# Two FFN blocks around a linear attention: part of five attentions done five phases later, Gelu factors and the residual sum on GpSimd, places for each engine

## What is computed

```python
x = x + 0.5 * ffn(layernorm(x))
x = x + linear_attention(layernorm(x))
x = x + 0.5 * ffn(layernorm(x))

def ffn(x):                       # the same weights both times
    q, k, v = heads(x @ Wq), heads(x @ Wk), heads(x @ Wv)      # 16 heads of 16
    attn = softmax(einsum('bqd,bkd->bkq', q, k) / sqrt(256))   # 1024 x 1024, over q
    z = unheads(einsum('bkq,bkv->bqv', attn, v)) @ Wo
    z = l2_normalize(l2_normalize(z) @ Wff)
    return gelu(z)

def linear_attention(x):          # 8 heads, no softmax
    q, k, v = (x @ w_qkv.T + b_qkv) split in three and by heads
    return ((q @ k.T) @ v) @ w_o.T + b_o
```

## Time and profile before

| | |
|---|---|
| median of three runs | 2874.6 us (2874.1 to 2875.76) |
| span of the profiled execution, first to last instruction | 2872.9 us |
| busy PE / DVE / ACT / POOL | 93% / 93% / 94% / 30% of the span |
| mean granted TensorE clock | 0.984 |
| phases 1 to 8 (with a linear attention) | 182.3 to 184.2 us each |
| phases 9 to 14 | 167.8 to 167.9 us each |
| phase 0, phase 15 | 165.0 and 162.8 us |
| ahead of the first tile, behind the last | 40.6 and 27.2 us |

### The profile page before, as it was taken

How to read it: one execution, slowest core, us unless ns; L and a number is a source line. 1 busy time by engine, 2 the same in 40 slices (tenths; PEclk the granted TensorE clock), 3 DMA queues, 4 the chain that set the end, 5 groups by cost and what they waited for, 6 DMA issues and landing times.

```text
span 2872.9 us, 87477 instructions
## 1 busy us (share of the span) xinstructions
PE 2670.2 (93%) x35680; PEld 1071.4 (37%) x35680; DVE 2667.4 (93%) x5390; ACT 2713.4 (94%) x5031; POOL 862.2 (30%) x1383
## 2 busy tenths in 40 slices
PE   6899999999999999999999999999989899899987
PEld 2233443434434344343443443333333333233432
DVE  5999998998989989999898999999999999999997
ACT  4999999999999999999999999999999999999998
POOL 2324204343143331432324313132331313233121
PEclk9999999999999999999999999999999999999999
DMA  5331242313422334123341243432324343232440
GB/s 125 55 80 30 50 102 53 81 33 60 105 40 53 74 60 104 32 54 81 60 98 30 51 92 60 92 61 57 79 45 103 60 90 61 51 87 43 89 89 16
DMA packets 151587, 192.90 MB, mean 67 GB/s; under 512 B 34129, under 2 KB 85841, under 8 KB 151186
## 3 DMA queue, kind: packets, MB, share of 16 engines
q1 hardware_dynamic: 150802, 186.52, 31.6%
q0 software_dynamic: 384, 0.79, 0.2%
HBM read 36.18 MB, written 16.78 MB: 18 GB/s over the span
## 4 chain that ended last, share of the span: by engine, by line
PE 35%; ACT 30%; DVE 27%; issue 6%; SPq 1%; DMA 0%; POOL 0%; DVEq 0%; ACTq 0%; POOLq 0%
ACT exp_ring L627 24%; DVE exp_ring L712 23%; PE ring L818 12%; PE ring L872 10%; PE o_acc L883 10%; ACT w_xn L638 2%; PE ring L928 2%; ACT xn_T L646 1%; ACT kq_stage L661 1%; DVE bn_stats L752 1%; ACT ring L633 1%; DVE w_xn L729 1%; ACT L638 1%; ACT L627 1%; DVE v_now L785 1%
## 5 line engine op out<-in xcount | busy, mean ns | idle before, releaser
L712 DVE TENSOR_SCALAR_CACHE_REDUCE exp_ring<-ring 128x1024 f32<-128x1024 f32 x2048 | 2409.7, 1214 | 114.4 <-PE ring L872 105.9
L627 ACT ACTIVATE exp_ring<-exp_ring,neg_max 128x1024 f32<-128x1024 f32 x2048 | 2333.0, 1143 | 84.6 <-DVE exp_ring L712 82.0
L872 PE MATMUL ring<-kq_stack 128*32 128x512 bf16 x16384 | 1176.0, 384 | 120.6 <-DVE exp_ring L712 82.1
L883 PE MATMUL o_acc<-exp_ring,v_scaled 128*32 128x512 f32 x8192 | 1080.1, 600 | 32.3 <-POOL v_scaled L580 22.7
L872 PEld LDWEIGHTS ring<-kq_stack 128*32 128x32 bf16 x16384 | 405.6, 96 | 1035.5 <-DVE exp_ring L712 415.7
L580 POOL TENSOR_TENSOR v_scaled<-v_now,exp_rsums 128x64 f32<-128x64 f32 x512 | 149.9, 293 | 1762.5 <-DVE exp_rsums L722 1745.2
L627 ACT ACTIVATION_READ_ACCUMULATOR exp_ring<-exp_ring,neg_max 128x1 f32 x2048 | 387.8, 189 | 0.0
L883 PEld LDWEIGHTS o_acc<-exp_ring,v_scaled 128*32 128x32 f32 x8192 | 252.5, 111 | 251.3 <-POOL v_scaled L580 40.1
L818 PE MATMUL ring<-ffn_wo_wowff,o_T 128*32 128x256 f32 x4096 | 244.2, 380 | 15.2 <-DVE o_T L719 13.9
L818 PE MATMUL ring<-xn_T,ffn_wqkv 128*32 128x512 f32 x2048 | 249.6, 608 | 8.1 <-DVE exp_ring L712 6.7
L818 PEld LDWEIGHTS ring<-ffn_wo_wowff,o_T 128*32 128x32 f32 x4096 | 132.3, 110 | 126.1 <-DVE exp_ring L712 26.1
(11 more groups left out here) (99 smaller groups left out, 1244.1 us busy)
## 6 DMA issues: line engine op xcount, KB each, us to landing
kq_stack<-kq_parts SPq DMA_DIRECT2D x2028, 64.0 KB, 2.4
x_post<-in_L_attn_x SPq DMA_DIRECT2D x8, 1024.0 KB, 8.8
x_slots<-x_post SPq DMA_DIRECT2D x8, 1024.0 KB, 5.5
x_prep<-x_slots SPq DMA_DIRECT2D x8, 1024.0 KB, 9.2
x_post<-x_slots SPq DMA_DIRECT2D x8, 1024.0 KB, 5.8
x_prep<-in_L_attn_x SPq DMA_DIRECT2D x7, 1024.0 KB, 9.1
out<-x_post SPq DMA_DIRECT2D x7, 1024.0 KB, 5.7
x_prep<-in_L_attn_x SPq DMA_DIRECT2D x2, 512.0 KB, 4.6
```

The lines of the kernel that those rows point to most:

```text
L627: nc.scalar.activation(e, e, ACT.Exp, bias=negmax[:, i % NM:i % NM + 1], scale=-1.0, accum_out=sums[:, g % EG, c:c + 1]).then_inc(exp_done, 1)
L712: nc.vector.tensor_scalar(E[:, (g % EG) * HQ + c, :].rearrange("p (b n) -> p b n", b=NB), ps, -1.0, None, ALU.mult, ALU.min, accum_out=neg ...
L872: last = mm(ps[k:k + COLS, n, :], kq[:, 0, c, j * P + k:j * P + k + COLS], kq[:, 1, c, n * BANK:(n + 1) * BANK], start=True, stop=True)
L883: last = mm(O[32 * c:32 * c + 32, n, :], vsc[a][:, g % EG, c, :], E[:, (g % EG) * HQ + c, n * BANK:(n + 1) * BANK], start=(a == 0 and j == ...
```

## The change

1. **Second parts later.** Batches 0 to 2 keep their linear attention in one phase (LINEAR, phases 1 to 3). For batches 3 to 7 phases 4 to 8 (FIRST) do it up to H; x_post (x1), H and the bias row are stored in DRAM, and the mean and factor of the second normalization stay in SBUF in one of six places. In phases 9 to 13 (SECOND), when x1 of the phase's own FFN is stored, SP loads x1, H and the bias of batch p-6; POOL normalizes again (`xn3`, the instruction of `xn2`), and `xt2`, `xbias`, `y` and the store follow (`save_y`). PLAIN is left for phases 0, 14 and 15.
2. **Gelu.** The factors are no longer ACT's scale: behind w_norm POOL multiplies w_xn by both factors, one instruction for each of 8 token tiles, and one Gelu instruction does 128 x 2048 (128 x 1024, twice, in the tail).
3. **Residual sum on POOL.** For each of four chunks it halves w_xn in place and adds it to x_post.
4. **Places.** Each engine has its own table of places, also for every single recip and av step; LEAD and GAP are gone. xt is copied by the engine in whose table it stands: DVE in FIRST, SECOND and PLAIN, ACT in START and LINEAR. z and v: ACT in LINEAR and FIRST, DVE in the others.
5. Small ones: the nbk row is gone, its product is done in T.

```diff
+    NOW = 3
+    LATER = B - 2
...
+LATE = ("load_x1", "load_h", "xn3", "xt2", "xbias", "y", "save_y")
...
+        if 1 <= p <= B:
+            return "LINEAR" if p <= NOW else "FIRST"
+        return "SECOND" if B < p <= PHASES - NOW else "PLAIN"
...
+        if kind in LATE and p > B:
+            return p - LATER
+        return p - 1 if p >= 1 else None
...
+            for kind, places in table(p).get(engine, {}).items():
+                parts = PARTS.get(kind, 1) if engine == "pe" else 1
+                for n, place in enumerate(places):
+                    q = work_of(kind, p, n // parts)
+                    if q is not None:
+                        placed.append((p * TILES + place, len(placed), (kind, q, n // parts), n % parts))
...
-    ON_ACT = {step for place, step in steps if step[0] in ("z", "v") and 1 <= place // TILES <= B}
+    ON_ACT = {step for step, _ in ORDER["act"] if step[0] in ("z", "v", "xt")}
...
+                elif kind == "save_x1":
+                    sp.wait_ge(x1_done, chunk(p, CHUNKS - 1))
+                    sp.dma_start(tokens(x1s[p]), xr[:]).then_inc(stored, 16)
+                elif kind == "load_x1":
+                    sp.wait_ge(stored, stored_before((kind, p, i)))
+                    sp.dma_start(xr[:], tokens(x1s[p])).then_inc(xr_loaded, 16)
+                elif kind == "save_h":
...
+                    sp.dma_start(hs[p], H[:].rearrange("p c d -> p (c d)")).then_inc(h_saved, 16)
+                    sp.dma_start(bs[p], biasw[:]).then_inc(h_saved, 16)
+                elif kind == "load_h":
...
+                    sp.dma_start(H[:].rearrange("p c d -> p (c d)"), hs[p]).then_inc(h_loaded, 16)
+                    sp.dma_start(biasw[:], bs[p]).then_inc(h_loaded, 16)
+                elif kind == "save_y" or kind == "store" and is_linear(p):
...
+                elif kind in ("xn2", "xn3"):
+                    if kind == "xn2":
+                        pool.wait_ge(rstd2_ready, (p + 1) * 2)
+                    else:
+                        pool.wait_ge(xr_loaded, xr_count("load_x1", p))
+                        pool.wait_ge(x1_done, chunk(p + LATER - 1, CHUNKS - 1))
+                    k = kept(p)
+                    nc.gpsimd.tensor_scalar(wb[:, i, 0:D], xr[:, i, :], negm2[:, k, i:i + 1], rstd2[:, k, i:i + 1],
                                             ALU.add, ALU.mult).then_inc(xn2_ready, 1)
...
-                    nc.gpsimd.tensor_tensor(gsc[:, c], ssw[:, c], unorm[:, c], ALU.mult).then_inc(norm_step, 1)
+                    for t in range(NT)[c]:
+                        nc.gpsimd.tensor_scalar(wb[:, t, 0:D], wb[:, t, 0:D], ssw[:, t:t + 1], unorm[:, t:t + 1],
+                                                ALU.mult, ALU.mult).then_inc(w_scaled, 1)
+                elif kind == "x1":
+                    rows = slice(i * CT, (i + 1) * CT)
+                    pool.wait_ge(gelu_done, chunk(p, i))
+                    nc.gpsimd.tensor_scalar(wb[:, rows, 0:D], wb[:, rows, 0:D], 0.5, 0.0, ALU.mult, ALU.add
+                                            ).then_inc(x1_half, 1)
+                    pool.wait_ge(xr_loaded, xr_count("load_xr", p))
+                    pool.wait_ge(x1_half, chunk(p, i))
+                    nc.gpsimd.tensor_tensor(xr[:, rows, :], xr[:, rows, :], wb[:, rows, 0:D], ALU.add
+                                            ).then_inc(x1_done, 1)
...
-                    act.wait_ge(norm_step, (p + i + 1) * 5)
-                    for c in range(NT)[norm_cols(p, i)]:
-                        last = nc.scalar.activation(wb[:, c, 0:D], wb[:, c, 0:D], ACT.Gelu,
-                                                    scale=gsc[:, c:c + 1])
...
+                    c = norm_cols(p, i)
+                    act.wait_ge(w_scaled, p * NT + c.stop)
+                    nc.scalar.activation(wb[:, c, 0:D], wb[:, c, 0:D], ACT.Gelu
+                                         ).then_inc(gelu_done, (c.stop - c.start) // CT)
...
-                elif kind == "x1":
-                    dve.wait_ge(xr_loaded, (p + 1) * 16)
-                    dve.wait_ge(gelu_done, chunk(p, i))
-                    rows = slice(i * CT, (i + 1) * CT)
-                    nc.vector.scalar_tensor_tensor(out=xr[:, rows, :], in0=wb[:, rows, 0:D], scalar=0.5,
-                                                   in1=xr[:, rows, :], op0=ALU.mult, op1=ALU.add
-                                                   ).then_inc(x1_done, 1)
...
+                elif kind == "xt" and (kind, p, i) not in ON_ACT:
+                    if p >= 1:
+                        dve.wait_ge(filled["qk"], nth("pe", "qk", p - 1, 7))
+                        dve.wait_ge(filled["v"], nth("pe", "v", p - 1, 3))
+                    nc.vector.tensor_copy(XT[:, i, :].rearrange("p (b n) -> p b n", b=NB), ps).then_inc(xt_out["dve"], 1)
```

581 lines of the change are left out of this document (393 added, 188 removed), and 50 rows, old and new, of the table TABLES.

## The result

The changed kernel takes **2801.53 us** (2799.59 to 2802.07, four runs) where the kernel before took 2874.35 us on the same chip: a ratio of 0.9747, 95% interval 0.9735 to 0.9758, or 72.8 us less. The forecast was 2834.6 us, with a range from 2805 to 2861. The time lies 3.5 us under the range, and the gain is nearly twice the 40.0 forecast.

A forecast was written before the change was run, and what follows sets the result against it. PE was taken to bound phases 1 to 8, ACT and DVE nearly equally 9 to 14. Terms -52.3 + 11.8 - 2.4 - 2 + 1 - 3 + 6.9 = -40.0 us from 2874.6 gave 2834.6, range 2805 to 2861.

The forecast's parts named there:

- The rival that POOL's queue becomes the bound: All phases: v_scaled late behind POOL's scalings and chunks, kernel slower, 2932 us with one more stall per phase; chance 0.05.
- Its price per stall, 6.5: One PE stall for v_scaled from POOL: 4.8 us of PE waiting plus 1.7 us of lowered clock.
- -52.3: Phases 4 to 8 together: 173.2 us each, 866.0 us against 918.3 us before.
- ACT 174.0 - 2.0 - 2.0 - 1.4 = 168.6: Phases 4 to 8: ACT's work, fullest engine, less two xt2 copies, two xT copies and the shorter Gelu, in us.
- I take 4.6: Phases 4 to 8: assumed idle us above the fullest engine, between 3.9 (phase 14) and 6.6 (phase 4), nearer to 3.9.
- With 4.4 above: 170.2 each: Phases 9 to 13: 4.4 us idle above DVE's 165.8; 851.0 us in all against 839.2, so +11.8.
- phase 14's 2.1 for the Gelu wait: Phase 14: DVE's 4.5 us idle less 2.1 waiting for Gelu, giving 165.5 us against 167.9, -2.4.
- What ACT and DVE lose had cover: Phases 1 to 3: PE keeps its work, so work taken off ACT and DVE was booked as no gain.
- up to 3 each: Phases 1 to 3: most us per phase from better v_scaled placement or its clock effect; 1 each booked, -3.
- Start-up: Before the first tile: steps reordered, none added; 0 us, between -1 and +2.
- edit (b): The residual sum, 2.7 us per phase, leaves DVE together with its wait for Gelu.
- the places fit well: All engines: waits and low clock vanish, 2.5 us idle, 2 us less in phases 1 to 3: 2808 us; chance 0.17.

The follow-up runs named there:

- the chain: Edits added in turn to the kernel before: places 2866.94 us, sum on POOL 2863.76, late-phase xT on DVE 2831.88, Gelu in one instruction 2813.31, move 2801.53.
- two later runs: Changed kernel with the last FFN's factor, Gelu and sum as before, 2794.11 us; the same with phase 14 by the places of SECOND, 2793.84 us.

## Why the prediction was wrong

**Right.** Phase 15 and the tail, to 0.2 us. The sizes of the instructions on POOL, ACT and DVE. The rival that POOL's queue becomes the bound did not come; v_scaled stands between the chunks, as it said, and PE waits 0.3 us for it in phase 4. Its price per stall, 6.5, was somewhat high: 4 to 5 in LINEAR. The loads of x1, H and bias had cover: in phase 12 neither POOL nor DVE waits for a DMA, and PE's one wait for kq_stack (1.1 us) is there without the move too (1.8).

**Right in sum, wrong in parts: phases 4 to 8** (-52.3, measured -49.7). By the runs it is places 2.7, sum 0.9, Gelu 1.4 and move 4.9 per phase, the last with the table FIRST and the xT copies in it. The 2.0 that the sum took off ACT for these copies were worth 0.1 per phase, by the run with the copies three tiles earlier on ACT. The step "ACT 174.0 - 2.0 - 2.0 - 1.4 = 168.6" measured 166.9, and "I take 4.6" for the idle time above the fullest engine measured 173.0 - 167.5 = 5.5 in phase 5, above PE. The two errors offset; that the total came out is partly luck.

**Wrong: phases 9 to 13** (+11.8, measured -9.2). The failed step is "With 4.4 above: 170.2 each". It took the idle time of DVE over as a property of three coupled engines. The work term of the fullest engine was near (DVE 165.8 against 164.9 in phase 12); the idle term was 1.5. PE's term was too large, 165.4 against 159.6: the moved work added 7.3 to the 152.3 of the run without it, not 10.0 to 155.4. Of the 4.5 us that DVE idled in phase 12 before, 2.9 were in-order waits for ACT: 2.1 for the Gelu, in ACT's stretch without exp, and 0.8 for exps, in two waits just behind ACT's two xT copies. The changed kernel has the sum on POOL, the copies on DVE and a stretch of 4.5 us for 5.9; both waits are gone, and DVE's wait for PE is 1.0 for 1.3. Shown: the Gelu's 1.4 us come through one for one where DVE, not ACT, is fullest (165.1 to 163.7 without the move, 167.9 to 166.5 with it), with the move 1.2 of them as DVE's wait for the sums; filler taken out of the stretch costs 2.9 per phase. Filler put in, together with ACT's relief, gives 3.5. Only phase 14's 2.1 for the Gelu wait was taken off; phases 9 to 13 have the same wait, so the sum was not even consistent with itself.

**Wrong: phases 1 to 3** (-3, measured -14.9). "What ACT and DVE lose had cover" failed. By the chain: places 8.0 (the v_scaled wait and the clock, of which I gave "up to 3 each" and took 1), Gelu 4.2, sum 2.7. PE was the fullest engine with 175.5 where it had no half clock (phase 6 before) and still is with 175.6 (phase 2 now), yet time that left ACT and DVE came off the phase.

**Start-up** (0, between -1 and +2; measured -2.1, and phase 0 -0.5 for +1). No run takes these 3.6 us apart.

**Why edit (b) looks good or bad.** The sum to POOL gives 3.2 us where xT is still on ACT, 24.6 to 49.3 where the other edits are in (by where on DVE it is put back), and in the kernel before, alone and in the late phases, costs 17. The Trainium skill (GPSIMD Engine Reference, Engine selection) says to leave two-input elementwise work to VectorE. The trace agrees on the price: a chunk costs POOL 1.8 us in two instructions and DVE 0.69 in one. In the changed kernel the measurement speaks against the rule, since POOL has the time. The 17 us in the kernel before don't speak for it: with the sum kept on DVE, only later, the late phases are the same 170.7.

**The rival "the places fit well"** had 2808 us, the nearest number, partly by another mechanism: it had 6 us in phases 1 to 3 and 21 in phases 4 to 13; the places alone gave 8.0 and 2.5 (13.7 off phases 4 to 8, 11.2 put on 9 to 13). How much of the late phases' 1.5 us of idle time is due to places made for these very edits can't be separated: each edit was undone at the new places, some of them (xT on ACT) poor ones for it.

## What to carry to other kernels

Idle time above the fullest engine is no constant to be carried from one version to the next: look up which in-order waits make it. Here one engine of the pipeline paused (ACT, for a function with a table load before and after it): 1.4 us less of the pause took 1.4 us off the phase, although another engine was fullest. Look what the partner has queued just there. Independent work is well placed there, a step that waits for the pausing engine is not; moving such work away, even off a full engine, slowed this kernel. When a copy changes engines, look what stands ahead of it in the queue: the xT copies on ACT cost 5.4 us in a late phase, behind the Gelu, and in phases 4 to 8 almost nothing once they stood three tiles earlier. Try edits of this kind together as well as alone: alone, the sum on POOL gave 3 us or cost 17, and beside the others 25 to 49.

## What the runs showed of the chip

- **The clock's part.** Mean granted clock was 0.984 before and 0.993 after. PE gaps of some us were followed by a few us at 0.50, the 1.2 GHz level (window above: 3.4 us at 444.6, behind gaps of 3.0 and 1.2 that end at 439.2 and 443.4). Where PE is the fullest engine the level has a price: phase 4 is 176.4 us with 3.4 of half clock and 174.8 without (two later runs with the same phases 1 to 13), phase 7 175.4 and 175.0 with it and 173.7 without. In the late phases of the kernel before none shows: phases 9 and 10 have 6.8 us of it, 11 to 13 have 3.4, and all take 167.8 to 168.0. With the sum on DVE beside the long Gelu phase 2 is 180.9 with no half clock; beside the short one it is 183.8 with 3.4 us of it. The wait of DVE for the Gelu is longer in the second, 1.4 us for 0.4, and so is PE's longest wait, 3.0 for 1.9; POOL's eight scalings of w_xn now stand ahead of this Gelu. Whether they are the reason, no run shows.
- **A shared port.** A chunk of the sum on DVE takes 0.68 us alone and took 1.09 beside POOL's 1.15 us instruction of two operands (rows of phase 2 above). By the Trainium skill (SBUF — State Buffer, Who interferes with whom) such a pair contends, and the trace agrees. With the sum on POOL that pair is gone; no run isolates what this is worth in the whole.
